# Attention outputs kept channel-major and normalized through DRAM and GpSimd, in place of TensorE transposes

## The reference, cut to what matters

```
energy = einsum('bqhd,bkhd->bhqk', q, k) * scale     # 16 heads of 8 channels, 512 tokens
attn   = softmax(energy (+ causal mask), axis=-1)
out    = einsum('bhqk,bkhd->bqhd', attn, v).reshape(b, s, 128)
return out @ W_out.T                                  # then residual and layer norm
```

## Time and profile before

| | us |
|---|---|
| median of 3 runs | 1388.23 (1387.31 to 1389.83) |
| the profiled execution | 1386.62 |
| its span, first to last instruction | 1384.8 |

### The profile page before, as it was taken

How to read it: one execution, slowest core, us unless ns; L and a number is a source line. 1 busy time by engine, 2 the same in 40 slices (tenths; PEclk the granted TensorE clock), 3 DMA queues, 4 the chain that set the end, 5 groups by cost and what they waited for, 6 DMA issues and landing times.

```text
span 1384.8 us, 26785 instructions
## 1 busy us (share of the span) xinstructions
PE 1218.0 (88%) x8190; PEld 650.1 (47%) x8190; DVE 932.8 (67%) x2502; ACT 710.5 (51%) x1300; POOL 269.9 (19%) x557
## 2 busy tenths in 40 slices
PE   3446999999889998999999999999999979999876
PEld 1222233333356655445555555556666535455445
DVE  5877778687455555767778776755554476668676
ACT  2221776777644434566666666663222227666643
POOL 3342211111000012322332332110000211222112
PEclk7557999999999998999999999999999989999988
DMA  7312232310000003323333222100000202221000
GB/s 207 124 65 73 87 90 68 120 35 19 1 1 1 0 1 120 105 66 107 106 98 126 74 78 76 45 4 3 1 0 0 74 12 67 77 81 40 2 1 31
DMA packets 65200, 79.16 MB, mean 57 GB/s; under 512 B 5483, under 2 KB 58068, under 8 KB 64602
## 3 DMA queue, kind: packets, MB, share of 16 engines
q1 hardware_dynamic: 65098, 77.89, 18.1%
HBM read 45.27 MB, written 31.72 MB: 56 GB/s over the span
## 4 chain that ended last, share of the span: by engine, by line
PE 62%; issue 13%; DVE 9%; ACT 4%; DMA 4%; DVEq 3%; POOL 2%; SPq 1%; POOLq 1%; ACTq 0%
PE bank L1606 11%; PE bank L1620 11%; PE bank L1590 9%; PE bank L1772 6%; PE bank L1773 6%; PE bank L1790 5%; PE bank L1574 3%; PE bank L1608 2%; DVE M L1189 2%; DMA KS<-scr_k 2%; PE bank L1640 2%; DVE masked_scores L1186 1%; PE bank L1510 1%; DVE N L1026 1%; PE bank L1570 1%
## 5 line engine op out<-in xcount | busy, mean ns | idle before, releaser
L912 ACT ACTIVATE PT<-bank 128x512 f32<-128x512 f32 (+1 forms) x784 | 427.5, 569 | 246.9 <-PE bank L1608 176.2
L1590 PE MATMUL bank<-KS,QS 125*128 125x512 bf16 (+3 forms) x1024 | 308.6, 329 | 31.5 <-DVE M L1186 12.1
L1606 PE MATMUL bank<-QS,KS 128*128 128x512 bf16 (+3 forms) x1024 | 303.7, 323 | 15.2 <-ACT PT L912 8.0
L1189 DVE TENSOR_REDUCE M<-bank 128x1 f32<-128x512 f32 (+2 forms) x400 | 257.8, 684 | 87.9 <-PE bank L1590 52.2
L1186 DVE CUSTOM_DVE_ANT_0 masked_scores<-bank,maskw 128x384 bf16<-128x384 f32 (+1 forms) x384 | 228.7, 622 | 90.0 <-PE bank L1590 78.8
L1620 PE MATMUL bank<-PT,VA 128*32 128x512 f32 (+3 forms) x2048 | 211.5, 485 | 1.6 <-ACT PT L912 1.0
L1606 PEld LDWEIGHTS bank<-QS,KS 128*128 128x128 bf16 x1024 | 99.3, 98 | 215.5 <-ACT PT L912 152.4
L1590 PEld LDWEIGHTS bank<-KS,QS 125*128 125x128 bf16 x1024 | 100.6, 99 | 109.0 <-DVE M L1189 31.9
L1608 PE MATMUL bank<-identb,maskw 128*128 128x128 bf16 x768 | 147.7, 219 | 0.0
L1790 PEld LDWEIGHTS bank<-MW,PT 128*128 128x128 f32 x864 | 111.7, 193 | 40.8 <-issue 38.2
L1772 PE MATMUL bank<-XT,MW 128*128 128x512 f32 (+1 forms) x232 | 120.7, 602 | 10.1 <-DVE PT L1363 5.9
(11 more groups left out here) (229 smaller groups left out, 1522.6 us busy)
## 6 DMA issues: line engine op xcount, KB each, us to landing
scr_q<-PQ SPq DMA_DIRECT2D x48, 384.0 KB, 3.2
QS<-scr_q SPq DMA_DIRECT2D x64, 288.0 KB
scr_k<-PK SPq DMA_DIRECT2D x24, 384.0 KB, 3.6
KS<-scr_k SPq DMA_DIRECT2D x32, 288.0 KB
QS<-MSB SPq DMA_DIRECT2D x192, 4.0 KB
MW<-in_m_w SPq DMA_DIRECT2D x3, 1024.0 KB, 9.5
MW<-in_m_w SPq DMA_DIRECT2D x3, 832.0 KB
scr_k<-PK SPq DMA_DIRECT2D x24, 96.0 KB, 1.9
```

The source lines that it names most:

```text
L912: a.activation(PT[kt % 2][:, js[0]:js[-1] + 1, q0:T], tiles(bank[st_bank(L, g, i)][:, 0:w * len(js)], len(js)), ACT.Exp, scale=c["scale"]) ...
L1189: v.tensor_reduce(M[g % 2][:, t * GH + js[0]:t * GH + js[-1] + 1], tiles(bank[S_ORDER[L][i]][:, 0:kl * len(js)], len(js)), AX_X, ALU.max, ...
L1590: r = mm(s, QS[0:ROWS_SHIFT, g * GH + j, t * P:(t + 1) * P], KS[0:ROWS_SHIFT, kv_slot(L, g, j), 0:kl], start=True, stop=not by_pe)
L1606: r = mm(s, KS[:, kv_slot(L, g, j), kt * P:(kt + 1) * P], QS[:, g * GH + j, T - w:T], start=True, stop=not causal)
```

## The change

The four helpers `o_t`, `ao_t`, `o_norm` and `ao_out` go, with their calls and with `last_ao`. OT stays channel-major. After each unit SyncE stores OT to DRAM (`store_o`, 256 KB). After the fourth unit of a block it loads the 16 heads' sums as a 128x64 tile and the outputs, packed to 128 channels, as OU (`load_o`); VectorE takes one reciprocal of 128x64 (`recip`); SyncE stores these (`store_recip`, 32 KB) and loads them spread over the channels (`load_recip`, 256 KB); GpSimd multiplies (`scale_o`) into AOT. In the SyncE unit `load_stack` of units 2 and 3 moves ahead, and the positions of the projection and what follows move back. The core of the diff:

```diff
-SHIFT_T_AT, O_OUT_AT, O_T_AT, O_NORM_AT, AO_T_AT, AO_OUT_AT = 3, 3, 6, 7, 9, 10
-Y_AT, Y_SUM_AT, Y_STATS_AT = (1, 1), (1, 4), (1, 6)
-LATER = dict(norm=(2, 2), stats2=(2, 5), norm2=(3, 3), xt=(3, 6), out=(3, 7))
-EARLIER = dict(norm=(2, 1), stats2=(2, 1), norm2=(2, 3), xt=(2, 6), out=(2, 7))
+LAST_R_AT, LAST_Y_AT, LAST_SUM_AT, LAST_NORM_AT, LAST_XT_AT, LAST_OUT_AT = 1, 5, 5, 7, 8, 8
+SHIFT_T_AT, O_OUT_AT = 3, 3
+RECIP_AT, Y_AT, Y_SUM_AT, Y_STATS_AT = (1, 0), (1, 9), (1, 10), (1, 10)
+LATER = dict(norm=(2, 3), stats2=(2, 5), norm2=(3, 3), xt=(3, 6), out=(3, 7))
+EARLIER = dict(norm=(2, 3), stats2=(2, 3), norm2=(2, 6), xt=(2, 8), out=(2, 9))
-LOGITS_AT, GATES_AT = {2: 0, 4: 1, 9: 2}, 9
-GATES_T_AT = {5: 0, 7: 1, 9: 2}
+LOGITS_AT, GATES_AT = {4: 0, 6: 1, 10: 2}, (3, 0)
+GATES_T_AT = {9: 0, 11: 1, 13: 2}
-LATE_LOGITS_AT, LATE_GATES_AT, LATE_T_AT = 6, 7, 11
+LATE_LOGITS_AT, LATE_GATES_AT, LATE_T_AT = 9, 9, 12
...
 # SyncE
+            def store_o(L, b, g):
+                sp.wait_ge(o_evac, U(L, b, g) + 1)
+                passed(b)
+                if g == 0:
+                    at_least(sp, o_landed, (b + NB * L) * 32)
+                    passed(b)
+                sp.dma_start(bass.AP(tensor=scr_o, offset=g * P * T, ap=[[T, P], [1, T]]), OT[:, :]).then_inc(o_stored, 16)
+            def load_o(L, b):
+                B = b + NB * L
+                sp.wait_ge(o_stored, (U(L, b, NG - 1) + 1) * 16)
+                passed(b)
+                at_least(sp, ao_ready, B)
+                passed(b)
+                sp.dma_start(sums[:, :], bass.AP(tensor=scr_o, offset=HD * T, ap=[[32 * T, H], [T // HD, HD], [1, T // HD]])).then_inc(o_landed, 16)
+                sp.dma_start(OU[:, :], bass.AP(tensor=scr_o, offset=0, ap=[[32 * T, H], [T, HD], [1, T]])).then_inc(o_landed, 16)
+            def store_recip(L, b):
+                B = b + NB * L
+                sp.wait_ge(recip_done, B + 1)
+                passed(b)
+                at_least(sp, recip_landed, B * 16)
+                passed(b)
+                sp.dma_start(bass.AP(tensor=scr_r, offset=0, ap=[[T // HD, P], [1, T // HD]]), recips[:, :]).then_inc(recip_stored, 16)
+            def load_recip(L, b):
+                sp.wait_ge(recip_stored, (b + NB * L + 1) * 16)
+                passed(b)
+                sp.dma_start(recips_wide[:, :], bass.AP(tensor=scr_r, offset=0, ap=[[T, H], [0, HD], [1, T]])).then_inc(recip_landed, 16)
...
                     if g == 0:
                         load_stack(L, b, 3)
+                    if g >= 2 and ahead:
+                        load_stack(ahead[0], ahead[1], g - 1)
+                    if prev:
+                        store_o(*prev)
                     if follow:
                         load_shift(*follow)
+                    if end and g == 0:
+                        load_o(*end)
                     if prep:
                         store_parts(*prep)
                         load_stack(*prep, 0)
-                    elif g >= 2 and ahead:
-                        load_stack(ahead[0], ahead[1], g - 1)
+                    if end and g == 1:
+                        store_recip(*end)
+                        load_recip(*end)
...
 # GpSimd
+            def scale_o(L, b):
+                B = b + NB * L
+                wait(o_landed, (B + 1) * 32)
+                wait(recip_landed, (B + 1) * 16)
+                wait(y_ready, b + NB * LAYERS[L]["phase"])
+                g.tensor_tensor(AOT[:, :], OU[:, :], recips_wide[:, :], ALU.mult).then_inc(ao_ready, 1)
...
                     if gg == 1 and end:
+                        scale_o(*end)
                         post_root(LAYERS[end[0]]["phase"], end[1])
...
 # ScalarE
             def o_out(L, u, g):
                 act.wait_ge(pv_done, (u + 1) * NT)
+                at_least(act, o_stored, u * 16)
                 a.activation(OT[:, :], bank[4][:, :], ACT.Copy).then_inc(o_evac, 1)
...
 # VectorE
+            def recip(L, b):
+                B = b + NB * L
+                dve.wait_ge(o_landed, (B + 1) * 32)
+                at_least(dve, recip_stored, B * 16)
+                v.reciprocal(recips[:, :], sums[:, :]).then_inc(recip_done, 1)
...
 # TensorE, unit
-                        if prev and i == O_T_AT:
-                            o_t(L, u - 1, u + 2 if follow else u + 1, not follow)
-                        if end and g == 0 and i == AO_T_AT:
-                            ao_t(*end, ...)
                         if end and (g, i) == Y_AT:
-                            pe.wait_ge(ao_evac, end[1] + NB * end[0] + 1)
+                            pe.wait_ge(prep_evac, preps_before(L, b))
+                            pe.wait_ge(ao_ready, end[1] + NB * end[0] + 1)
                             y_out(AOT, attn_weights(end[0])[5], end[1], LAYERS[end[0]]["phase"])
```

More of the change, by code:

```diff
@@ L562, in unit @@
                         load_stack(*prep, 0)
-                    elif g >= 2 and ahead:
-                        load_stack(ahead[0], ahead[1], g - 1)
+                    if end and g == 1:
+                        store_recip(*end)
+                        load_recip(*end)
                 sequence(L, unit, sp.Fori)
+                if ends_chain(L):
+                    store_o(L, NB - 1, NG - 1)
+                    load_o(L, NB - 1)
+                    store_recip(L, NB - 1)
+                    load_recip(L, NB - 1)
             attention_sp(0)
@@ L749, in body @@
                         wait(gt_evac, b * 2 + 2)
-                        wait(y_ready, b + NB * p)
+                        if not is_first(b):
+                            wait(y_ready, b + NB * p)
                         g.tensor_copy(RWB[:, :], blk(RW9, b)).then_inc(rwb_ready, 1)
@@ L758, in body @@
                     if is_first(b):
+                        scale_o(BEFORE[p], NB - 1)
                         post(LAYERS[BEFORE[p]]["phase"], NB - 1)
@@ L782, in ffn_root @@
                 g.tensor_tensor(FRSTD[:, :], FVE[:, :], neg_half[:, :], ALU.pow).then_inc(fr_ready, 1)
+            ffn_root(0)
+            scale_o(3, NB - 1)
             post_root(L3_ATTN, NB - 1)
[L785 removed]
+            ffn_root(1)
             post_save(L3_ATTN, NB - 1)
[L787 removed]
             for b in range(2, NB):
@@ L921, in unit @@
                             m_out(*follow)
-                        if end and g == 0 and i == AO_OUT_AT:
-                            ao_out(*end)
                         if end and (g, i) == end_at(L, b)["out"]:
                             xt_out(LAYERS[end[0]]["phase"], end[1])
-                        if L in GATED_BY and is_last(b) and (g, i) == (2, GATES_AT):
+                        if L in GATED_BY and is_last(b) and (g, i) == GATES_AT:
                             gate_exp(GATED_BY[L], 0)
@@ L1228, in unit @@
                                 prep_dve(*prep, at[i])
-                        if prev and i == O_NORM_AT:
-                            o_norm(*prev, u - 1)
+                        if end and (g, i) == RECIP_AT:
+                            recip(*end)
                         if end and (g, i) == Y_SUM_AT:
@@ L1627, in shift_t @@
                 pe.wait_ge(m_split, w + 1)
-                pe.wait_ge(o_normed, w - 1) if not isinstance(w, int) or w > 1 else None
+                at_least(pe, m_evac, w)
                 to = bank[7][0:PARTS * GH, 0:T // 2].bitcast(BF16)
@@ L1632, in shift_t @@
                 r.then_inc(mt_ready, 1)
-            def o_t(L, u, shifts, last=False):
-                pe.wait_ge(o_evac, u + 1)
-                pe.wait_ge(m_evac, shifts)
-                if last:
-                    pe.wait_ge(o_normed, u + 1)
-                for t in range(NT):
-                    r = tr(bank[7][:, t * P:(t + 1) * P], OT[:, t * P:(t + 1) * P], ident[:, :])
-                r.then_inc(ot_ready, 1)
-            def ao_t(L, b, preps):
-                pe.wait_ge(o_normed, U(L, b, NG - 1) + 2)
-                at_least(pe, prep_evac, preps)
-                for t in range(NT):
-                    r = tr(bank[6][:, t * P:(t + 1) * P], AO[:, t, :], ident[:, :])
-                r.then_inc(ao_ready, 1)
             def attention_pe(L):
@@ L1774, in up @@
                     if p == L1_MOE:
+                        if c == 0 and is_first(b):
+                            pe.wait_ge(o_evac, U(L, NB - 1, NG - 1) + 1)
                         if c == 0 and is_last(b):
```

110 lines of the change are left out of this document (50 added, 60 removed).

## The result

The changed kernel takes 1503.77 us (median of 4 runs, 1501.25 to 1505.37) against 1387.77 us for the kernel before on the same chip: 1.0834 times as long, 95% interval 1.0812 to 1.0857. So it is slower, as forecast, but by 116 us where the forecast had 74, and above the range of 1400 to 1490. The profiled execution has a span of 1503.6 us, where before it was 1384.8.

What follows compares the result with a forecast made beforehand. TensorE's issue time plus its waits was taken to bound the kernel. From 1386.62 us, -37 (removed), +64 (projection wait), +28 (shift wait), +16 (clock) and +3 (gate transpose) gave +74, 1460 us; range 1400 to 1490.

Steps and rivals of the forecast that it cites:

- the removed slots: TensorE's output transposes (28.2 us), transposes back (7.0) and small waits (2) go: 37 us less, bounds 30 and 45.
- the wait at the projection: Unit 1, item 9: TensorE waits for the reciprocals' DMAs and GpSimd's multiply, 4.9 us in 13 blocks: +64, bounds 52 to 85.
- the second wait: Unit 2, causal blocks: the shift's transpose waits for GpSimd's shift, now behind the root, 2.8 us in 10 blocks: +28.
- clock around the 13 stalls: TensorE's clock halves for 3.4 us after each projection stall, losing 1.2 us each: +16 us, bounds nothing and 49.
- gate transpose, first MoE: In the first MoE the gate transpose waits about one chunk more for the last gate step: +3 us.
- FFN: The sum moves one step on VectorE and the reciprocal's wait lies where it waited for GELU: 0, within 3.
- A step that leaves TensorE is worth its slot: In attention, TensorE busy 99.79 of 100 us was taken to bound the time, so removed TensorE time counts in full.
- rival of a covered projection: Unit 1, item 9: the projection's wait is covered, so only the removal's 37 us counts: 1350 us; chance 0.10.
- The 6.5 to 7 us given for two blocks of attention 1: SyncE is already behind there, so two blocks' projections were to stall longer than 4.9 us.
- The load's bound: The reciprocals' 256 KB load into SBUF: 2.3 us from a store of that size, bounds 1.9 and 3.2.
- The rival: Long clock falls: each projection stall brings 10.2 us of half clock, +33 on the sum, 1493 us; chance 0.08.
- The cover in the experts layers: At chunk 5 the projections come after the DMA chain, 13 us against some 17 of chunks, and cost nothing.

Runs made afterwards that it cites:

- e4: Kernel before without the output transposes, `o_norm`, transposes back and `ao_out`; projections multiply a constant table, no DMA added: 1368.41 us.
- e3: Changed kernel with GpSimd doing the shift ahead of the statistics' root in unit 1: 1484.24 us.
- e12: Changed kernel with 28 useless matmuls on TensorE ahead of the wait for the scaled outputs, in 13 attention blocks: 1490.03 us.
- e8: Changed kernel with the 13 attention projections multiplying a constant table, and GpSimd's unit 1 ordered shift, root, multiply: 1384.04 us.
- e5: Changed kernel with the reciprocals' store and load issued on ScalarE's queue, at items 1 and 5 of unit 1, instead of SyncE's: 1428.49 us.
- e1: Changed kernel with the 13 attention projections multiplying a constant table without waiting; the DMA chain and GpSimd's multiply still run: 1427.36 us.
- e10: e7 with the last block's normalization through gates one chunk earlier in experts layers, and the FFN's last-block projection after the first four hidden-layer transposes: 1392.78 us.
- e7: Changed kernel with e5 and e3 together, the projection one item later, its normalization, transpose and evacuation one or two later: 1389.22 us.

## Why the prediction was wrong

Direction and mechanism were right: the projection stalls 13 times behind the reciprocals' way through DRAM, the shift behind the root on GpSimd, and the clock falls. The sum was too small by 43 us. Two of its terms lie outside their own bounds: the removed slots, 19 us against 37 (30 to 45), and the wait at the projection, 87 us against 64 (52 to 85). A third miss, the second wait, went the other way and hid 10 us. Term by term; what no run measures is the last row but one:

| term | predicted, us | measured, us | by |
|---|---|---|---|
| transposes removed | -37 | -19 | e4 |
| wait at the projection | +64 | +87 | the 13 stalls in the trace after |
| wait at the next shift | +28 | +18 | its group after; e3 gives 19.5 with its clock |
| clock around the 13 stalls | +16 | +19 | e12 |
| gate transpose, first MoE | +3 | +2 | last exponential of attention 0 to the first of attention 1, before and after |
| FFN | 0 | +5 | last exponential to the end, before and after |
| not attributed | | +5 | what is left of the sum |
| sum | +74 | +117 | 1503.77 less 1386.62 |

**The removed slots: the first step that failed.** "A step that leaves TensorE is worth its slot" was read from 99.79 busy of 100. The prediction itself put 30 as the lower end; 19 is below it. A causal unit gained 0.23 us for a slot of 0.44, since ScalarE's exponentials were only 0.2 us behind. Busy time of a pipelined engine doesn't tell by how much it leads the next. Its own test ("if units without a block end do not get shorter by 0.4 us") came out: bare causal units went from 9.74 to 9.51 us after the change too. This error also sits in the rival of a covered projection: it gave 1350, and e8, where the 13 projections wait for nothing, is at 1384.

**The wait at the projection: the largest miss, in the instruction named but not in its size.** From the end of `m_out` to the projection the prediction had 7.3 us, and the trace of this block has 12.2 (870.52 to 882.70): 5.1 in place of 1.8 until SyncE issues the store, 2.0 for its landing (1.9 predicted), 3.6 in place of 2.3 for the load, 1.4 in place of 1.3 for the multiply. TensorE in turn wants it 3.7 us behind `m_out` and not 2.4. So 12.2 - 3.7 = 8.45 where 7.3 - 2.4 = 4.9 stood. The same over all 13 blocks:

| mean of 13 blocks, us | predicted | measured |
|---|---|---|
| end of `m_out` to the issue of the reciprocals' store | 1.8 | 3.6 |
| that store's issue to the load's | 1.9 | 1.8 |
| the load's issue to the multiply | 2.3 | 3.5 |
| multiply to the projection | 1.3 | 1.4 |
| less: end of `m_out` to where TensorE is out of work | 2.4 | 3.7 |
| stall | 4.9 | 6.7 |

The load's excess and TensorE's later need cancel. The latter is a slip in the prediction's own working: it moved TensorE's need forward by the 0.99 us of the old projection, but that one stood ahead of `m_out` as well, so both move. What is left, 1.8 us in the mean and 23 us over 13 blocks, is the time until SyncE issues the store: 1.3 because the shift goes out late, 0.5 for SyncE's own issues around it. The step that failed is that the shift was taken to be issued at `m_out`'s end, as the earlier trace rows showed it for this block before. In five of the 13 blocks it was (0.02 to 0.03 us behind), and these have the stalls of 4.56 to 5.76; in the other eight it came 0.8 to 4.5 us late. SyncE's queue in the block shown before the change, ahead of the earlier trace rows:

```profile
816.24 1.40 SPq L515 DMA_DIRECT2D scr_k<-PK  x3
819.50 0.31 SPq L525 DMA_DIRECT2D QS<-scr_q  x1
```

There the parts' store began 3.87 us ahead of `m_out` (820.11), and the stack loads, which wait for its landing, were out just before its end. After the change it began 2.38 us ahead (867.57 to 869.95): the units are 1.5 us shorter up to this place, the chain that makes the parts is not. That and a landing later by 0.5 us keep SyncE until 872.11, 1.6 us behind `m_out`'s end. The outputs' store takes it to the shift at 872.96, the shift to 874.97, and 0.66 us pass before the reciprocals' store goes out. The prediction named the gain of the removed slots and did not move SyncE's schedule against it. The 6.5 to 7 us given for two blocks of attention 1 stand against 10.21, 8.77 and 6.74. e5 settles the cause: with the same transfers, no quicker, on a queue without this order, 75 us go.

The load's bound was taken from a store of the same size, 2.3 us. The loads took 3.3 and 3.5 us in the median. The estimate from the Trainium skill, "DMA: Bandwidth & Descriptors", "Anatomy of one DMA", was 2.1 and 2.6 us for the pair, 4.7 in all; measured are 2.0 and 3.6, 5.6 in all. It was nearer than my sum, and still short by the load. The rule of the Trainium skill to issue early and wait late ("DMA: Bandwidth & Descriptors", "Rules for kernel authors") is what the change breaks, and e5, which issues both earlier, puts a price on it: 75 us.

**The wait at the shift** was right in mechanism and place, nine times where ten were forecast, and of 1.5 to 2.3 us mostly (once 3.7), not 2.8. Part of the delay probably lies in the first stall's shadow, where VectorE's maxima had ended and the sum and the statistics can start at once. e1 shows the other side: without the first stall the second wait is 37 us.

**The clock** around the 13 stalls was nearly right, 18.6 us (15 to 23) against 16, in part by luck: the forecast had 3.4 us at half clock for each stall and 1.2 of it lost. The trace has 3.4 us twice, 6.8 nine times and 10.2 and 13.7 once each, much of it inside the stall, and 1.4 lost for each. The rival had 3.8 lost for each, 49 in all.

**FFN: 0 was wrong.** I named GELU as the cover of the wait. The reciprocals' two landings are behind the last outputs, and the projection stands ahead of the transposes and waits 6.60 us. The 5.46 us ahead of the transposes did go, so that much was covered, and still the stretch is 4.7 us longer; the clock is at half there for 13.7 us where it was for 10.2. e10 tried one other order, and it was worse: there the transposes waited 7.67 us for VectorE themselves.

**The cover in the experts layers** held: the projection at chunk 5 waits for nothing.

Where the 14 to 16 us between e8 and e4 lie is open beyond the 7 us of the ends of the chains. e7 has the normalization two items later: unit 2 then costs 0.9 us over the kernel before, but unit 1 12.8. Another order of VectorE's work in these units was not tried. None of the versions that compute the same result is measurably faster than the kernel before.

## What to carry to other kernels

Before a dependent DMA is added to a queue, write down everything that the queue's engine issues and waits for ahead of it; the time from data ready to data back is set there. Here two transfers of 2.0 and 3.6 us became a chain of 14 us (868.27 to 882.70), and moving them to an engine that was at the right point of its program gave back 75 of 116 us without a change to the transfers. And before an engine's removed slot is counted in full, look at what its next instruction would have waited for: take the work out alone and time it. Here this showed 19 us where 37 were counted, and a change that adds waits in 13 places has to stay under 1.5 us in each to be worth 19.

## What had not been expected of the hardware

- A 256 KB load from DRAM into SBUF took 3.3 and 3.5 us to landing (medians), a 256 KB store 2.0 us here and 2.3. The two loads pack or repeat rows on their way and the stores don't; no run tells the direction from the pattern.
- The stretches at half clock differ in length from stall to stall, and 12 of the 13 begin inside the stall. These are windows of the changed kernel: in the stall of 10.21 us (647.55 to 657.75) the clock is 0.50 from 650.00 on, and stays there for 13.7 us, of which the last 5.9 lie behind the stall's end with TensorE at work.

```profile
650.00:663.70 13.70, 5.61 (x35) 4.20 (x37) 2.06 (x6) 1.00 (x2) 1.26 (x1) 0.50 0.26 76
657.80:663.70 5.90, 5.57 (x35) 4.12 (x37) 2.06 (x6) 1.00 (x2) 0.00 (x0) 0.50 0.25 70
```

  Around the stall of 8.45 us (874.26 to 882.70) it is at half for 6.8 us, from 878.71 to 885.54, and the row of the projection lasts 2.04 us in place of 1.16. Filling the stalls with matmuls of no use made the kernel 13.7 us faster.
